# Four token groups in flight in the first attention stage, each with its own PSUM banks and buffers

## The reference

```python
qkv = einsum('bnm,om->bno', x, w_qkv)             # x normalised over its features before
q, k, v = split into 16 heads of 8
dots = einsum('bhid,bhjd->bhij', q, k)
norm = sqrt(sum(dots * dots, axis=-1, keepdims=True))
attn = dots / maximum(norm, EPS) * norm_g + norm_b
out = einsum('bhij,bhjd->bhid', attn, v)
y = einsum('bnm,om->bno', out, w_out) + b_out      # y is normalised, then added to x
```

## Time and profile before

| | us |
|---|---|
| median of three runs | 2512.11 |
| lowest and highest | 2511.95, 2513.39 |
| profiled execution | 2515.83 |
| its span in the trace | 2513.9 |
| TensorE busy over the span | 2312.5 (92%) |
| VectorE busy | 1766.0 (70%) |
| ScalarE busy | 1373.6 (55%) |
| GpSimd busy | 1598.5 (64%) |

### The profile page before, as it was taken

One profiled execution on the slowest core, in us unless ns is written; L12 is line 12 of the kernel. 1 busy time (PEld: TensorE's weight loads), 2 busy tenths in 40 slices (PEclk: granted clock), 3 DMA queues, 4 the chain that ended last, 5 costly groups with the idle time before them and its releaser, 6 DMA issues.

```text
span 2513.9 us, 81640 instructions
## 1 busy us (share of the span) xinstructions
PE 2312.5 (92%) x34944; PEld 1575.0 (63%) x34944; DVE 1766.0 (70%) x2707; ACT 1373.6 (55%) x2778; POOL 1598.5 (64%) x931
## 2 busy tenths in 40 slices
PE   5668999999999999999999999999987988889998
PEld 3435666666666666666666666666655766656665
DVE  2348788877888778887788778887756888832232
ACT  1115666666666666666666666666644666643332
POOL 0039889888898888888888888988843222201111
PEclk8879999999999999999999999999987899989999
DMA  4001111111121112211121112211122000000000
GB/s 111 0 9 37 30 35 51 49 43 30 34 58 50 33 32 51 53 37 31 33 62 48 33 30 58 52 33 35 30 58 64 1 1 1 1 1 5 5 5 5
DMA packets 77303, 83.91 MB, mean 33 GB/s; under 512 B 24964, under 2 KB 48786, under 8 KB 76946
## 3 DMA queue, kind: packets, MB, share of 16 engines
q1 hardware_dynamic: 76946, 78.70, 12.2%
HBM read 26.56 MB, written 1.07 MB: 11 GB/s over the span
## 4 chain that ended last, share of the span: by engine, by line
PE 49%; DVE 29%; issue 12%; ACT 7%; POOL 3%; SPq 0%; ACTq 0%; DMA 0%; POOLq 0%; DVEq 0%
PE bank L613 7%; DVE n L1222 6%; DVE qk L1215 6%; PE bank L532 5%; ACT qk L908 4%; PE bank L625 4%; PE sbank L569 3%; PE bank L633 3%; DVE sh L1235 3%; DVE mx L1231 3%; PE bank L821 2%; PE obank L831 2%; PE sbank L831 2%; PE obank L602 2%; PE sbank L821 2%
## 5 line engine op out<-in xcount | busy, mean ns | idle before, releaser
L1215 DVE TENSOR_TENSOR qk<-bank,tab 128x1024 f32<-128x1024 f32 x384 | 469.2, 1222 | 212.5 <-ACT qk L908 212.4
L1528 POOL TENSOR_TENSOR qk<-qk 128x1024 f32<-128x1024 f32 x192 | 454.3, 2366 | 188.5 <-DVE qk L1215 188.3
L1532 POOL TENSOR_TENSOR rn<-n2m,cst 128x16 f32<-128x16 f32 x192 | 562.8, 2931 | 16.0
L532 PE MATMUL bank<-wqk,xs 128*128 128x512 f32 x768 | 409.2, 615 | 2.6 <-DMA xs<-Z 0.9
L908 ACT ACTIVATE qk<-bank 128x512 f32<-128x512 f32 x384 | 226.5, 590 | 300.5 <-PE bank L532 300.5
L1536 POOL TENSOR_TENSOR qk<-qk,rn 128x1024 f32<-128x1024 f32 x192 | 365.4, 1903 | 28.1 <-POOL rn L1532 0.9
L543 PEld LDWEIGHTS bank<-cst,qk 128*128 128x128 f32 x1536 | 191.5, 141 | 215.6 <-issue 170.4
L1540 POOL TENSOR_TENSOR lnr<-lnv,cst 128x2 f32<-128x2 f32 (+1 forms) x88 | 66.4, 754 | 394.1 <-DVE lnv L1110 394.1
L543 PE MATMUL bank<-cst,qk 128*128 128x128 f32 x1536 | 231.8, 274 | 11.3 <-POOL qk L1536 11.3
L1222 DVE TENSOR_REDUCE n<-qk 128x16 f32<-128x1024 f32 x192 | 232.1, 1209 | 0.0
L553 PE MATMUL lnbank<-wv,xs 128*64 128x512 f32 x768 | 208.0, 620 | 0.0
(11 more groups left out here) (201 smaller groups left out, 4332.6 us busy)
## 6 DMA issues: line engine op xcount, KB each, us to landing
vp<-vp SPq DMA_DIRECT2D x672, 65.0 KB, 2.0
wqk<-in_L_ffn_Wqkv SPq DMA_DIRECT2D x24, 256.0 KB, 3.7
wv<-in_L_ffn_Wqkv SPq DMA_DIRECT2D x6, 512.0 KB, 4.0
wo<-in_L_ffn_Wo SPq DMA_DIRECT2D x6, 512.0 KB, 4.2
xs<-Z SPq DMA_DIRECT2D x48, 64.0 KB, 2.0
xs<-Z SPq DMA_DIRECT2D x48, 63.8 KB, 2.7
vp<-in_L_ffn_w SPq DMA_DIRECT2D x1, 2048.0 KB, 13.1
mw<-in_L_ffn_w SPq DMA_DIRECT2D x8, 256.0 KB, 6.9
```

The costliest lines, as they stand in the source:

```text
L532: nc.tensor.matmul(bank[s % 2][:, :], xs[:, odd, WIN + r * P:WIN + r * P + P], wqk[:, lo:lo + 512], start=True, stop=True).then_inc(p_full, 1)
L1215: tt(qk[:, both, :].rearrange("p o (h d) -> p o h d", d=DH), heads(bank[c % 2][:, :]).unsqueeze(1).broadcast_to([P, 2, PAIRS, DH]), table. ...
L1528: tt(direct, direct, swapped, ALU.add).then_inc(sum_done, 1)
L1532: tt(rn[:, m % 2, :], n2m[:, :], const("mhalf"), ALU.pow).then_inc(rn_done, 1)
```

## The change

The stage is cut into 18 visits for each group. In round s, every engine makes visit s of group 0, visit s-2 of group 1, visit s-4 of group 2 and visit s-6 of group 3, so that there are 24 rounds. Each group owns two of the eight PSUM banks (`one`, `two`) and six buffers of 512 columns. They lie in memory that later stages use (`mw2`, `qT`, `aoT`, `sh`, `px`, `pT`, `ao`). With two banks for a group, the projections of k and v are done in two visits. The masks and the tables are made by VectorE between visits of round 10, 12 and 14. The SyncE queue waits for the last norm of the group that a batch belongs to, in place of `z_ready`, and TensorE waits for all twelve norms before it writes the masks.

```diff
+GROUPS1, VISITS1, APART1 = B // 2, 18, 2
+NORMS1 = (1, 12, 15)
+ORDER1 = [(j, slot - APART1 * j) for slot in range(VISITS1 + APART1 * (GROUPS1 - 1)) for j in range(GROUPS1)
+          if 0 <= slot - APART1 * j < VISITS1]
...
+        homes = ((mw2f[:, 0:1024], mw2f[:, 1024:2048], mw2f[:, 2048:3072]),
+                 (mw2f[:, 3072:4096], qTf[:, 0:1024], qTf[:, 1024:2048]),
+                 (shf, aoTf[:, 0:1024], aoTf[:, 1024:2048]),
+                 (pTf, pxf, aof))
...
-                wait(sp, z_ready, t + 1)
+                if t < B:
+                    sp.wait_ge(ln_done, unit1(b // 2, 2) + 1)
+                else:
+                    wait(sp, z_ready, t + 1)
...
 # TensorE; one, two = the group's banks
+                if k == 0:
                     for i in range(4):
+                        mm = nc.tensor.transpose(one[:, i * P:i * P + P], xin[:, 4 * j + i, :], ident)
+                if k == 1:
+                    mean1(group(X, j), two)
+                if k == 2:
+                    var1(j, 0, two)
+                if k == 3:
+                    wide1(j, 0, two)
+                if k == 4:
+                    nc.tensor.matmul(one[:, :], w1t[:, 0:P], s1a[j], start=True, stop=True)
+                    for i in range(2):
+                        mm = nc.tensor.matmul(two[:, i * 256:i * 256 + 256], s1a[j][:, i * P:i * P + P], w1t[:, P:3 * P],
...
+                if k == 5:
                     pe.wait_ge(s1["sb"], j + 1)
+                    for i in range(2):
+                        mm = nc.tensor.matmul(one[:, i * 256:i * 256 + 256], s1a[j][:, 256 + i * P:256 + i * P + P], w1t[:, P:3 * P],
...
+                if k == 6:      # k times k and v, 4 + 4 matmuls into two and one
+                if k == 7:      # 2 matmuls, into one
+                if k == 8:      # 1 matmul, into two
+                if k == 10:     # 2 matmuls, into one
+                if k == 11:     # output projection, into two
+                if k == 12, 13, 14: mean1, var1, wide1 of the second norm, in one
+                if k == 15, 16, 17: the same of the third norm, in two
+            for j, k in ORDER1:
+                visit1(j, k)
...
             pe.wait_ge(masks_cast, 1)
+            pe.wait_ge(ln_done, LN_S2)
...
 # ScalarE
+                if k == 0:      # copy to X;  k in NORMS1: square
+                if k == 4:      # copies of q and of half of k and v;  k == 5: of the other half
+                if k == 8:      # square root;  k == 10: scale and bias;  k == 11: bias
...
 # VectorE
+                if k == 9:
                     dve.wait_ge(s1["nr"], j + 1)
+                    nc.vector.reciprocal(s1c[j], s1d[j]).then_inc(s1["rn"], 1)
                     dve.wait_ge(s1["rn"], j + 1)
+                    tt(s1f[j], s1b[j], s1c[j], ALU.mult).then_inc(s1["qg"], 1)
...
+            for j, k in ORDER1:
+                visit1(j, k)
+                if j == 0 and k == 10:
+                    dve.wait_ge(ld_tables, 32)
+                    nc.vector.tensor_copy(ident_bf, ident)
+                    nc.vector.tensor_copy(maskv, work[:, 2]).then_inc(masks_cast, 1)
+                if j == 0 and k == 12:
+                    dve.wait_ge(ld_vec, 16 * 11)
+                    tables(0)
+                if j == 0 and k == 14:
+                    tables(1)
```

More of the change, by code:

```diff
@@ L443, in _ @@
             pe.wait_ge(s3["ub"], 1)
[L444 to L472, removed]
[L473 to L475 removed]
+            def mean1(src, b):
+                nc.tensor.matmul(b[:, :], onesm, src, start=True, stop=True).then_inc(ln_mean, 1)
@@ new lines, in var1, with wide1 @@
+            def var1(j, n, b):
+                pe.wait_ge(ln_sq, unit1(j, n) + 1)
+                for i in range(4):
+                    mm = nc.tensor.matmul(b[:, 2 * i:2 * i + 2], s1d[j][:, i * P:i * P + P], onesm[:, 0:2], start=True, stop=True)
+                mm.then_inc(ln_var, 1)
+            def wide1(j, n, b):
+                pe.wait_ge(ln_rstd, unit1(j, n) + 1)
+                for i in range(4):
+                    mm = nc.tensor.transpose(b[:, i * P:i * P + P], s1lnr[:, j, i:i + 1].broadcast_to([P, P]), ident)
+                mm.then_inc(ln_wide, 1)
@@ L503, in attend1 @@
                     mm.then_inc(s1["o"], 1)
-                if slot == 7:
+                if k == 11:
                     pe.wait_ge(s1["os"], j + 1)
[L506 to L515, removed]
+                    nc.tensor.matmul(two[:, :], w1t[:, 3 * P:4 * P], s1a[j], start=True, stop=True).then_inc(s1["y"], 1)
@@ new lines, in visit1 @@
+                if k == 12:
+                    pe.wait_ge(s1["ys"], j + 1)
+                    mean1(s1b[j], one)
+                if k == 13:
+                    var1(j, 1, one)
+                if k == 14:
+                    wide1(j, 1, one)
+                if k == 15:
+                    pe.wait_ge(s1["x1"], j + 1)
+                    mean1(group(X, j), two)
+                if k == 16:
+                    var1(j, 2, two)
+                if k == 17:
+                    wide1(j, 2, two)
@@ L866, in _, with square1 @@
             act.wait_ge(ld_s1, 80)
[L867 to L876, removed]
-                    act.wait_ge(s1["qkv"], j + 1)
[L878 to L882, removed]
+            def square1(j, n):
+                act.wait_ge(ln_d, unit1(j, n) + 1)
+                nc.scalar.activation(s1d[j], s1c[j], ACT.Square).then_inc(ln_sq, 1)
@@ new lines, in visit1 @@
+                if k == 12:
+                    centre1(s1b[j], j, 1, one)
+                if k == 13:
+                    eps1(j, 1, one)
+                if k == 14:
+                    out1(s1e[j], j, 1, one)
+                    dve.wait_ge(ln_done, unit1(j, 1) + 1)
+                    tt(x, x, s1e[j], ALU.add).then_inc(s1["x1"], 1)
+                if k == 15:
+                    dve.wait_ge(s1["x1"], j + 1)
+                    centre1(x, j, 2, two)
+                if k == 16:
+                    eps1(j, 2, two)
@@ L1192, in _, with tables @@
+                if k == 17:
+                    out1(group(Z, j), j, 2, two)
             rotc = const("rot").rearrange("p (k r d) -> p k r d", k=4, r=2)
-            for k in range(2):
+            def tables(k):
                 scale = scales[:, k, :, :]
```

176 lines of the change are left out of this document (86 added, 90 removed).

## The result

| | before | changed |
|---|---|---|
| median, 4 runs each | 2512.68 us | 2446.68 us |
| lowest to highest | 2511.95 to 2513.39 | 2443.92 to 2447.86 |
| span of the profiled execution | 2513.9 | 2445.9 |
| ratio (95% interval) | | 0.9735 (0.972 to 0.9751) |

The changed kernel is 66 us faster. The gain is a fifth larger than the 54 us forecast. The second comparison's median lies inside the range; what separates the two is treated at the end of the experiments.

What follows compares the result with a forecast made beforehand. The stage was taken as bound by a chain of engine hand-overs, no engine full. Stage 149.1 to 97 us plus 1.8 of hand-over saves 53.9, forecasting 2458 us; 8-in-10 range 2447 to 2474.

Steps and rivals of the forecast that it cites:

- the tables: Made by VectorE in rounds 12 and 14: cost nothing in 12 and 1.2 us in 14, already in the sum.
- the hand-over: Between the stage's last norm and TensorE's first projection: 2.94 us shrinks to about 1.1, saving 1.8 us.
- cold clock throughout: Rival 1, the stage: TensorE stays at 1.2 GHz in all rounds, 12.4 us saved, 2500 us; chance 0.05.
- engines in turns: Rival 2, the stage: engines alternate instead of overlapping; 2543 us at 1.2 GHz, chance 0.04, or 2483 at 2.4, 0.04.
- a gain that does not reach the end: Rival 3, behind the stage: something fixed, such as layer 0's weights, holds the time at 2512 us; chance 0.02.
- Rival (4): The stage: rounds are no walls and 2.4 GHz holds almost throughout, so 86 us and 2447 in total; chance 0.13.
- the head: Rounds 0 to 5: 14.9 us at 2.4 GHz, 22.8 at 1.2; taken at 1.2 GHz for about half.
- the tail: Rounds 18 to 23: 14.0 us at 2.4 GHz, 21.2 at 1.2; taken at 1.2 GHz for about half.
- the sum of the rounds: The stage's 24 rounds: 88.9 us at 2.4 GHz, 96.4 with slower ends, taken as 97 with falls, against 149.1.
- start to start of neighbours: TensorE's prices at 2.4 GHz: 0.96 us per 512-column matmul, 1.05 per variance, 0.59 per four transposes.
- the wall: Every round costs the largest of TensorE's sum, VectorE's sum and the longest chain; 88.9 us over 24 rounds at 2.4 GHz.
- the Trainium skill's rule on transposes: Last twelve rounds: transposes do not count as busy for the clock, so 1.2 GHz lasts longer, 97 + 7 = 104 us.

Runs made afterwards that it cites:

- second comparison: The changed kernel run again against the kernel before, on one chip: 2449.21 against 2512.61 us, ratio 0.9748.
- e5: Changed kernel with only the SyncE queue's wait for z_ready put back: 2451.76 us, ratio 0.9758 to the kernel before; hand-over 2.95 us.
- e6: Changed kernel with each group's reciprocal replaced by a multiplication by one, output scale left wrong: median 2442.28 us, stage 85.0 against 87.8.
- e9: Changed kernel plus filler matmuls on TensorE in the first and last rounds: stage 87.9 us, ratio 0.9729 to the kernel before.
- e11: Changed kernel with groups one visit apart, tables at the tail and filler matmuls: 2441.21 against 2513.91 us before, ratio 0.9714; stage 80.7.
- e15: Same kernel as the changed one with groups one visit apart, tables at the tail and fillers, traced again: stage 80.5 us.

## Why the prediction missed

Right, and shown: the stage was a chain and became dense; the gain's direction; the hand-over (1.8 forecast, 2.0 in the trace, and undone alone by e5); the loads were done, for no engine waited for them; the six layers kept their time; the clock at 2.4 GHz in the middle and 1.2 at the end. The rivals with a cold clock throughout, with engines in turns, and with a gain that does not reach the end did not happen. Rival (4), no walls and hardly any 1.2 GHz, with its 2447, was nearest, and I gave it 0.13. It was right about the walls, but not about the clock: the head, 4 us near 79 and the tail were at 1.2 GHz.

The step that failed is the sum of the rounds, 97 us where 87.8 were measured. By stretches, with the second column an estimate by the prediction's own rule (of a round's engines and chains the longest), with TensorE's time for rounds 4, 6, 7, 8 and 10 from the changed kernel's trace (3.05, 5.6, 3.0, 6.0, 6.2) and the prices above for the others:

| rounds | forecast | with dense prices, 2.4 GHz | measured |
|---|---|---|---|
| 0 to 5 | 18.9 | 14.4 | 16.5 |
| 6 to 11 | 32.9 | 30.9 | 27.8 |
| 12 to 17 | 27.1 | 25.6 | 25.4 |
| 18 to 23 | 17.6 | 13.9 | 18.0 |
| falls between | 0.6 | | |
| all | 97.1 | 84.8 | 87.7 |

First, the prices: my "start to start of neighbours" came from places with a wait in them. The mean of 81.60 had itself just waited 0.67 us, and costs 0.96 instead of 0.86. Behind the variance of 65.38 the next matmul waited for VectorE up to 66.43: 1.05 instead of 0.81. The four transposes had waited for GpSimd, and I took 0.06 for their overlap: 0.59 instead of 0.43. These prices were too high by a tenth to a third, worth 2.0 + 1.5 us in the middle. Second, the wall: a round was taken as the largest of three sums, and the 24 largest were added. Engines drift by a round when the waits allow it, so VectorE's long round 9 or 11 and TensorE's long round 10 lie beside each other. That is worth 3.1 us in rounds 6 to 11; e6 shows it, where TensorE had no gap left. In rounds 12 to 17 this gain and a fall hide each other: round 13 took 2.7 us instead of 4.9, but round 16, at 1.2 GHz, 4.8 instead of 3.6. For falls I had put 0.6 us in all; this one alone cost 1.8 by the dense prices, which give round 16 3.0. Third, the head: I charged half of the cost of 1.2 GHz there, 18.9 in all; the projection at 26.27 already takes 1.02, so rounds 4 and 5, where TensorE has most to do, were at 2.4 GHz already, and the head took 2.4 less, 0.5 of it by the prices. The tail was charged nearly rightly. Of the tables I had priced only VectorE's own time, 1.2 us; the wait that they bring to TensorE stood in no term. e9 shows that even these figures hang on where a fall comes.

The 3 to 5 us behind the layers are outside every term I had. They are likely chance in part, as said, and the second comparison, 63 us, is what the stage and the hand-over explain (61.4 + 2.0). By these two alone the forecast's own steps give 2513.9 - 63.4 + 1.9 - 3.7 = 2448.7, inside the range. So it took what was gained behind the layers to carry the time out of the range, while the 9 us of the stage were my error.

The stage by the Trainium skill's rule on transposes, which the prediction weighed (TensorE: Matmul & The Clock Gate, Part 4: PE-mode transpose), would have been 104, farther off than the forecast. The tail was indeed at 1.2 GHz, but TensorE also waited there (12.5 us from 90.50, 8.43 busy), so the trace decides nothing about the rule.

## What to carry to other kernels

When several groups are put in flight, price the busy engine from a stretch where it had no waits at all; a gap hidden inside a start-to-start time grows with every instruction. Add engines' totals over a few rounds and not the largest of each round, since in-order engines that wait only for their own group's last visit drift apart and fill each other's long rounds. And give each end of the pipeline its own sum: there the chain rules, closer starts shorten it (two visits apart to one: 3.9 us), and work that is needed only later, as the tables here, belongs there: in the middle, behind a long instruction of the same engine, it can make the busy engine wait (1.94 us here).

## What the runs showed of the hardware

The same four groups' instructions on TensorE took 75.7 us busy when interleaved and 130.3 when run one group after the other, at granted clocks of 0.91 and 0.59 as the column gives them. Two executions of one kernel had different falls: e11 shows 1.00 over its stage, e15 0.98 with 1.2 GHz from about 63 to 66, and behind the layers the two differ by 9.3 us. A filler that helps at one place (1.7 us in the head of e9) can be followed by a fall elsewhere that takes it back. Differences of 5 us between two kernels of this kind need several traces before they are given to the edit.
